# A graph network kernel: order of work in the mixing stage, bias by matrix product in the relation stage

## The reference, cut to what matters

```python
# layer 1, last lines: weighted sum of the sources' features per target, then elu
h_prime = segment_sum(attention[:, None] * h[src], dst, num_segments=num_nodes)
return elu(h_prime)
# layer 2
rel = node_type[edge_src] * (T * R) + node_type[edge_dst] * R + edge_type
all_msgs = einsum('ni,moi->nmo', x, W)
msg = all_msgs[edge_src, rel]
agg = segment_sum(msg, edge_dst, num_segments=n_nodes)
out = agg + bias
```

## Time and profile before

| what | value |
|---|---|
| median of 3 runs | 7306.34 us (7302.04 to 7308.86) |
| profiled execution | 7280.67 us, span 7278.9 us |
| VectorE busy over the span | 5486.2 us (75%) |
| TensorE busy over the span | 3968.5 us (55%) |
| mixing stage, first load to last result | 4573.9 to 4905.8 us |
| relation stage, first gather to last result | 4911.3 to 5550.6 us |

### The profile page before, as it was taken

The page is one execution under the profiler, slowest core; times in us unless marked ns, Lnnn a source line. Parts: engine busy times, 40 slices in busy tenths (PEclk is TensorE's granted clock), DMA queues, the critical chain, the costliest instruction groups (busy, mean ns, idle before and its releaser), DMA issues. The chain is left out here.

```text
span 7278.9 us, 83566 instructions
## 1 busy us (share of the span) xinstructions
PE 3968.5 (55%) x13024; PEld 2369.0 (33%) x13024; DVE 5486.2 (75%) x16937; ACT 3171.6 (44%) x7568; POOL 4455.4 (61%) x4321
## 2 busy tenths in 40 slices
PE   0002666664665665997000989876886766773000
PEld 0000332322333334886000545672332433331000
DVE  4502898986777777887777999776887888886886
ACT  0001666663333333776444000124554666665555
POOL 2777777775777776775776000007664777774776
PEclk9999677776888887555555989558997676665555
DMA  6001555555333332212998000459884555554554
GB/s 190 4 1 34 99 98 98 100 98 81 87 85 84 86 85 61 49 47 57 121 118 102 2 5 1 136 150 129 155 152 108 116 113 115 113 115 110 169 167 136
DMA packets 905930, 687.04 MB, mean 94 GB/s; under 512 B 595425, under 2 KB 744702, under 8 KB 905180
## 3 DMA queue, kind: packets, MB, share of 16 engines
q1 hardware_dynamic: 517168, 403.39, 20.5%
q0 software_dynamic: 137984, 138.92, 18.9%
q10 hardware_dynamic: 250600, 143.02, 6.5%
HBM read 491.06 MB, written 227.24 MB: 99 GB/s over the span
## 5 line engine op out<-in xcount | busy, mean ns | idle before, releaser
L1793 POOL DMA_INDIRECT f_dg<-t_D,c_at x392 | 379.7, 969 | 1132.5 <-POOLq L179 943.3
L802 POOL DMA_INDIRECT b_xg<-t_H,c_at x784 | 828.4, 1057 | 286.0 <-issue 238.6
L802 POOL DMA_INDIRECT g_xg<-t_D,c_at x784 | 801.7, 1023 | 319.9 <-issue 237.7
L802 POOL DMA_INDIRECT a_xg<-t_XL,c_at x784 | 824.6, 1052 | 250.1 <-issue 238.7
L2181 POOL DMA_INDIRECT out<-n_yo,c_at x392 | 430.8, 1099 | 237.5 <-issue 116.0
L440 POOL DMA_INDIRECT t_XL<-su_pos,su_scatx x392 | 388.2, 990 | 244.7 <-DMA t_XL<-in_nodes 125.7
L1326 POOL DMA_INDIRECT l_d<-t_D,l_ix x392 | 399.3, 1019 | 174.8 <-issue 115.8
L1141 POOL DMA_INDIRECT t_RANK<-m_place,m_at x392 | 400.8, 1022 | 160.9 <-issue 115.7
L938 ACT ACTIVATE a_hn<-a_xg,a_sm 128x64 f32<-128x64 f32 x784 | 269.9, 429 | 399.0 <-DVE a_sm L675 398.0
L1375 ACT ACTIVATE l_hn<-l_xs,l_sm 128x64 f32<-128x64 f32 x784 | 265.0, 426 | 284.0 <-DVE l_sm L675 218.9
L2160 ACT ACTIVATE n_h<-n_x,n_sm 128x64 f32<-128x64 f32 (+1 forms) x800 | 269.4, 426 | 210.0 <-DVE n_sm L675 210.0
(11 more groups left out here) (451 smaller groups left out, 13667.4 us busy)
## 6 DMA issues: line engine op xcount, KB each, us to landing
a_ends<-t_LAST SPq DMA_DIRECT2D x98, 256.0 KB
t_XSD<-a_xg SPq DMA_DIRECT2D x98, 256.0 KB
t_H<-a_oE ACTq DMA_DIRECT2D x98, 256.0 KB
b_ends<-t_LAST SPq DMA_DIRECT2D x98, 256.0 KB
l_xb<-t_XSD SPq DMA_DIRECT2D x49, 512.0 KB
f_rl<-t_REL SPq DMA_DIRECT2D x49, 512.0 KB
g_xb<-t_XSD SPq DMA_DIRECT2D x98, 256.0 KB
g_ends<-t_LAST SPq DMA_DIRECT2D x98, 256.0 KB
```

The costliest lines, as they stand in the source:

```text
L802: nc.gpsimd.indirect_dma_start(xg[k][:, j, i, :], None, table, bass.IndirectOffsetOnAxis(ap=C["at"][:, i, n * J + j:n * J + j + 1], axis=0 ...
L1793: nc.gpsimd.indirect_dma_start(dg[k][:, u, j, :], None, T["D2"], bass.IndirectOffsetOnAxis(ap=C["at"][:, 0, (2 * n + u) * J + j:(2 * n + u ...
```

## The change

In the mixing stage two lists are put in another order. VectorE now runs `product` at the head of its step, ahead of `result` and `sums`; the chunks that each call handles in a step stay the same. ScalarE now runs `store` at the end of its step, behind `negative` and `exponents`. SyncE's list and its waits are unchanged.

In the relation stage the addition of the bias on VectorE (`d2b`, L1855) goes. The running sums get a row more, filled with ones once ahead of the steps, and `turn_back` becomes a matrix product of 65 rows with `turn_bias`: the identity with the bias below it. It is no transpose any more, and each product is two instructions on TensorE, as those of `project` are (784 for 98 chunks of four, where `turn_back` had 392 for 49 steps of eight). `result` adds `d2` to `b_back` directly.

```diff
--- before.py
+++ after.py
@@ -1675,7 +1675,7 @@
                 v.scalar_tensor_tensor(o[k][:, :, :], t[k][:, :, :], -1.0, dd[k][:, :, :], ALU.add, ALU.add
                                        ).then_inc(s_o, 1)
                 ch.done()
-            flow(dve, [(4, result), (2, sums), (1, product)], slots=SL)
+            flow(dve, [(1, product), (4, result), (2, sums)], slots=SL)
 
         @block.tensor
         def _(pe):
@@ -1710,7 +1710,7 @@
             def store(n, k, q, old):
                 act.wait_ge(s_o, n + 1)
                 act.dma_start(rows(T["D2"], n), o[k][:, :, :]).then_inc(s_st[k], 16)
-            flow(act, [(4, store), (3, negative), (3, exponents)], slots=SL)
+            flow(act, [(3, negative), (3, exponents), (4, store)], slots=SL)
             for k in four:
                 act.wait_ge(s_st[k], 16 * chunks_of(k, SL))
 
@@ -1738,9 +1738,9 @@
         rl = [m.sb(f"rl{k}", [P, 2, CH]) for k in two]
         kp = [m.sb(f"kp{k}", [D, 2, CH]) for k in two]
         d2 = [m.sb(f"d2{k}", [P, 2, J, D]) for k in two]
-        d2b = m.sb("d2b", [P, 2, J, D])
         sel = [[[m.sb(f"sel{k}{u}{g}", [P, CH]) for g in two] for u in two] for k in two]
-        ag = [m.sb(f"ag{k}", [D, 2, CH]) for k in two]
+        ag = [m.sb(f"ag{k}", [D + 1, 2, CH]) for k in two]
+        turn_bias = m.sb("turnbias", [D + 1, D])
         o = [m.sb(f"o{k}", [P, 2, J, D]) for k in two]
         srow = m.sb("srow", [1, D])
         bn = m.sb("bn", [P, G, 6])
...
@@ -1800,11 +1800,12 @@
         def _(dve):
             v = nc.vector
             for k in two:
-                last = v.memset(ag[k][:, :, :], 0.0)
-            last.then_inc(s_end, 1)
+                v.memset(ag[k][0:D, :, :], 0.0)
+                v.memset(ag[k][D:D + 1, :, :], 1.0)
+            v.tensor_copy(turn_bias[0:D, :], C["ident"][0:D, 0:D])
+            v.tensor_copy(turn_bias[D:D + 1, :], C["bias2"][D:D + 1, :]).then_inc(s_end, 1)
             dve.wait_ge(s_end, 1)
-            ch, cho = Chain(dve, s_ch, 2 + LN_OPS), Chain(dve, s_cho, 1)
-            b2 = C["bias2"][:, :].unsqueeze(1).to_broadcast([P, G, D])
+            ch = Chain(dve, s_ch, 2 + LN_OPS)
             flat = lambda t: t.rearrange("p u j d -> p (u j) d")
 
             def norm(n, k, q, old):
@@ -1841,23 +1842,18 @@
                     dve.wait_ge(s_b, n - 1)
                 for u in two:
                     dve.wait_ge(s_m, 2 * n + u + 1)
-                    before = ag[1 - k % 2][:, 1, CH - 1:CH] if u == 0 else ag[k % 2][:, 0, CH - 1:CH]
+                    before = ag[1 - k % 2][0:D, 1, CH - 1:CH] if u == 0 else ag[k % 2][0:D, 0, CH - 1:CH]
                     if u or later(n):
                         dve.wait_ge(s_ag, 2 * n + u)
-                    v.tensor_tensor_scan(ag[k % 2][:, u, :], kp[k % 2][:, u, :], b_m[u][0:D, :], before,
+                    v.tensor_tensor_scan(ag[k % 2][0:D, u, :], kp[k % 2][:, u, :], b_m[u][0:D, :], before,
                                          ALU.mult, ALU.add).then_inc(s_ag, 1)
 
             def result(n, k, q, old):
-                cho.at(n)
                 dve.wait_ge(s_d2[k % 2], 16 * counted(n, k, q))
-                if later(n):
-                    dve.wait_ge(s_o, n)
-                cho(v.tensor_tensor(flat(d2b[:, :, :, :]), flat(d2[k % 2][:, :, :, :]), b2, ALU.add))
                 dve.wait_ge(s_b, n + 1)
                 if later(n, 2):
                     dve.wait_ge(s_st[k % 2], 16 * (counted(n, k, q) - 1))
-                v.tensor_tensor(o[k % 2][:, :, :, :], d2b[:, :, :, :], b_back[:, :, :, :], ALU.add).then_inc(s_o, 1)
-                cho.done()
+                v.tensor_tensor(o[k % 2][:, :, :, :], d2[k % 2][:, :, :, :], b_back[:, :, :, :], ALU.add).then_inc(s_o, 1)
             flow(dve, [(5, result), (3, select), (4, sums), (1, norm)], total=NB, slots=SL)
 
         @block.tensor
@@ -1894,8 +1890,8 @@
                     hold(pe, s_pturn, (s_o, n))
                 for u in two:
                     for j in range(J):
-                        last = nc.tensor.transpose(b_back[:, u, j, :], split(ag[k % 2][:, u, :])[:, :, j],
-                                                   C["ident"][0:D, 0:D])
+                        last = nc.tensor.matmul(b_back[:, u, j, :], split(ag[k % 2][:, u, :])[:, :, j],
+                                                turn_bias[:, :], start=True, stop=True)
                 last.then_inc(s_b, 1)
             first_half, second_half = ((lambda n, k, q, old, fn=fn, u=u: fn(n, k, u)) for fn, u in ((vectors, 0), (vectors, 1)))
             first_sum, second_sum = ((lambda n, k, q, old, u=u: compose(n, k, u)) for u in two)
```

More of the change, by code:

```diff
@@ L1754, in relation_block @@
         s_rl, s_kp, s_d2, s_st = (m.sems(x, 2) for x in "rl kp d2 st".split())
-        s_xs, s_n, s_f, s_hn, s_t, s_h, s_v, s_sel, s_m, s_ag, s_b, s_o, s_ch, s_cho, s_turn, s_end, s_pturn = (
-            m.sem(x) for x in "xs n f hn t h v sel m ag b o ch cho turn end pturn".split())
+        s_xs, s_n, s_f, s_hn, s_t, s_h, s_v, s_sel, s_m, s_ag, s_b, s_o, s_ch, s_turn, s_end, s_pturn = (
+            m.sem(x) for x in "xs n f hn t h v sel m ag b o ch turn end pturn".split())
         block = ctx.enter_context(nc.Block())
```

## The result

| | before | after |
|---|---|---|
| median | 7307.60 us (4 runs, 7302.04 to 7313.52) | 7675.68 us (4 runs, 7671.41 to 7689.89) |
| ratio, 95% interval | | 1.0507 [1.0489, 1.0525] |
| profiled execution, its span | 7280.67, 7278.9 us | 7672.5, 7670.7 us |
| mixing stage, first to last result | 319.7 us | 555.8 us |
| relation stage, first to last result (L1859, now L1856) | 584.2 us | 733.5 us |

The change makes the kernel 5.1% slower. The two stages together lost 236 + 149 = 385 us between the two traces; 230 were forecast, 220 and 10.

The account below looks back on a forecast made before the run. No engine was full: mixing hid its load's trip under VectorE work, relation followed a two-step ring. Mixing +220 and relation +10 on the profiled 7280.7 gave 7511, plus 25.7 to the runs' median 7536 us; range 7490 to 7578.

Parts of the forecast that it names:

- 94 x 2.34 = 220: Mixing stage: 94 steps whose load waits for a result each grow 2.34 us, from 3.30 to 5.64, 220 us.
- The ring: Mixing stage: load waits for result, product for load, result follows product; trip plus three VectorE instructions, 5.64 us a step.
- the trip from the end of the result to the product, 4.42 us: Mixing stage: time for a buffer's next load to reach its product, taken between 4.35 and 4.49 us.
- the trip shortens: Mixing stage rival, 6%: lighter traffic makes the load's trip a tenth shorter, 7496 us, or a fifth, 7449.
- The bias sum at nothing: Relation stage: removing VectorE's bias sum, some 0.72 us a step, gains nothing because it stands beside the ring of two steps.
- 0.23 each, so 0.12 at 1.00 if it follows the clock: Relation stage, turn_back: price of each of sixteen weight loads, taken from project's 1.97 us for eight at clock 0.50.
- The row is nearer to 0.96: Relation stage: of the bounds for turn_back's added time, nothing and 0.96 us a step, the row lies nearer the latter.
- Ring or TensorE: Relation stage: a ring of two steps through turn_back sets the step, 11.75 to 12.43 us; TensorE alone would need 11.69.
- The half way between 11.75 and 12.43: Relation stage: step taken as 12.1 to 12.15 us, between no half-clock stretches and the clock as it is.
- the clock drops in every step: Relation stage rival, 12%: longer turn_back lowers the clock each step, TensorE needs 13.05 us, +41, with the end +44, 7570.
- relation gains: Relation stage rival, 10%: VectorE is the bound, so dropping the bias sum saves 27 us, 7499.
- the other side of zero: Mixing stage rival, 3%: load no hindrance, VectorE not waiting for exponentials, kernel up to 52 us faster, 7264.

Follow-up runs that it names:

- head_only: Kernel before with only VectorE's product moved to the head of its mixing step, store and relation stage as before: 7517.38 us in one run.
- store_only: Kernel before with only ScalarE's store moved to the end of its mixing step: 7285.26 us, 1.0007 [0.9997, 1.0016].
- rel_transpose: Kernel before without the relation stage's bias sum, turn_back still by transposes, bias left out of the output: 7275.06 us, 0.9997 [0.9987, 1.0006].
- rel_keep_sum: Changed relation stage with a zero bias row in the product and VectorE's bias sum kept, mixing stage as before: 7423.85 us, one run.
- rel_contig: Changed relation stage with turn_back reading 128 neighbouring columns instead of every fourth, mixing stage as before: 7313.43 us, one run.
- split_head: Kernel before with the changed mixing lists and three of four loads released earlier, after the running sum: 7217.35 us, 0.9916 [0.9899, 0.9932].
- rel_only: Kernel before with only the relation stage changed, mixing stage as before: 7428.95 us, 1.0201 [1.0181, 1.0221].
- rel_rows64: Changed relation stage with turn_back a product of 64 rows, without the bias row, mixing stage as before: 7437.96 us, one run.

## Why the prediction was right and wrong

**The direction** and the size of the mixing stage were right; the total was 140 us short and outside the range, and nearly all of it is one term of the relation stage.

**Mixing, 94 x 2.34 = 220: right, a little small.** Measured 236. The ring is what was described: SyncE's wait 94 times, the product's 98 times 3.3 us against "about 3 us each", the exponentials' wait gone (2.2 us left); only the total, 325.5 us, lies above "260 to 290". The part from a waiting product to the end of the result was 1.22 in the step shown, as predicted, and 1.24 on average. The mis-sized term is the trip from the end of the result to the product, 4.42 us; it is 4.51 in the step shown and 4.60 on average. Both rows it was taken between lay below that, the upper one, 4.49, nearer. One step is a thin base: over its 94 loads the trace of before has a median of 4.46 us from the end of the result to the landing of the last transfer, above the 4.35 of the step that was read. `head_only` and `store_only` confirm that the place of the product is what costs, and that the late store costs nothing that the runs can tell.

**The rival "the trip shortens"** is refuted: traffic fell from 160 to 91 GB/s, and from the end of the result to the last landing the median went from 4.46 to 4.54 us. By the estimate from the Trainium skill, DMA: Bandwidth & Descriptors, section "Anatomy of one DMA", the trip would be 4.02; this trace doesn't agree: from the last issue at 4812.81 to the product alone it is 2.78 us, where the estimate had 2.3. The page gives that figure for the path of GpSimd's transfers, and these are SyncE's.

**The bias sum at nothing: right.** "It stands beside the ring, so nothing is gained from it" is what `rel_transpose` and `rel_keep_sum` measured.

**`turn_back`, "0.23 each, so 0.12 at 1.00 if it follows the clock": this step failed.** It doesn't follow the clock. The row used, `project` at clock 0.50, gives the same 0.23 as `turn_back` at 1.00. I had both numbers, 0.12 for a transpose at full clock and 0.23 for a product at half, and halved the second because it then met the first. The transposes themselves could have warned: in the trace of before they are 0.12 apart at clock 1.00 and at 0.50 alike, so neither of the two strided loads had been seen to follow it. `rel_contig` shows that the halving holds for columns that lie side by side, 0.11 at 1.00 against 0.21 at 0.50, and not for those four floats apart. So sixteen add 3.81 - 1.03 = 2.78 us a step and not 0.96: this is the term that was mis-sized, and at its true size it is TensorE's own time and not the ring that sets the step. "The row is nearer to 0.96" was wrong; the 2.7 at the other end, tied there to the half clock, was the right price at either. That end was named and then not carried into the stage's upper bound of +23; through TensorE's own time it gives (12.09 + 2.7 - 11.97) x 48 = 135 us, and with the trip of 4.6, +237, the range would have ended at 7306 + 237 + 135 = 7678 and held the result. Why a transpose reads the same columns at 0.12 no run here tells. The Trainium skill, TensorE: Matmul & The Clock Gate, section "LDWEIGHTS (loading the stationary operand)", has 107 ns with no word of the clock. The strided product keeps one price at either clock, but it is 0.23 us; side by side it comes near, 0.11, at 1.00 alone, and takes 0.21 at 0.50 (`rel_contig`).

**A smaller slip.** The prediction multiplied what a step gains or loses in the relation stage by 38, the steps in the window of the earlier trace rows; the stage has 48 from its first to its last result. With 48 its 0.17 us are 8 us and not 7, its +41 for the clock 52. That is a few us beside the 140 that are missing.

**Ring or TensorE.** The half way between 11.75 and 12.43 has no meaning any more: TensorE's own time, 12.09 from turn to turn in the earlier trace rows, plus 2.78 is 14.87, above the ring's (23.89 + 2.78)/2 = 13.3. TensorE became the bound, all but the 0.86 us in which `turn` waits for ScalarE's copy, and the step took 15.35, beyond the 12.6 from which the prediction called itself wrong. The 0.5 that is left over 14.87 I put down to the clock: the first `vectors` takes 3.65 us on average instead of 3.34, and every other first `compose` 2.85 instead of 1.93. Of the 3.38 us a step that were lost against 11.97, 2.78 are the instructions. The first `vectors` and `compose` are 0.97 + 0.45 = 1.42 longer by the clock; that is more than the 0.6 left, since TensorE's idle time fell too, from 1.46 to 0.85 us a step. No run held the clock fixed. **The rival "the clock drops in every step"** thus did happen, and was given 12%; but its +44, 7570, lies 106 us below the result.

**The rival "relation gains"** and the other side of zero didn't show. What the latter needed, "the load would have to be no hindrance", is what `split_head` gave it, and it came out at -65 us, near the -52 worked out there. That nearness is in part luck: the -52 took VectorE's four instructions for the limit, and in `split_head` it is TensorE that is busy all the time.

## What to carry to other kernels

Before an instruction is moved ahead in a loop, look which buffer it reads and what has to run before that buffer's load may start: if that stands right ahead of it in the new order, the whole trip of the load becomes part of every step, and its present wait of nearly nothing says only how much cover it has now. A price read at one clock may be scaled to the other only if the same operation with the same stride is seen to follow it; when the row is at hand, take its own number as one bound of the sum. And where an order makes a load late, release the parts of the load separately, each at its own last reader, before giving the order up.

## What the runs showed of the hardware that was not expected

- Weight loads of 128 float32 columns for a product, from one to the next: 0.23 us at clock 1.00 and at 0.50 when the columns are four floats apart, with 65 rows (after, `rel_only`) or 64 (`rel_rows64`), and 0.23 in `project` at 0.50; side by side 0.11 at 1.00 and 0.21 at 0.50 (`rel_contig`). The transposes of before, with the same stride, 0.12 at either.
- In the mixing stage of `split_head` TensorE was busy 210.00 of 210.00 us, by modelled ends, with transposes and 64-column products, and the clock stayed at 0.50, the 1.2 GHz level.
- From the end of the result to the landing of the last of the four transfers it took 4.46 us before, at 160 GB/s, and 4.54 after, at 91, each the median of the stage's 94 loads.
